# A selective scan's broadcast rows issued ahead of its state sums, the skip term at step 8, and the gate multiply ahead of step 2's multiply

## The reference

```
dt = softplus(einsum('blr,dr->bld', dt, W_dt) + b_dt)
dA = exp(dt[..., None] * A)                        # b, s, 256, 16
dBu = dt[..., None] * Bm[:, :, None, :] * u[..., None]
h_t = dA_t * h_{t-1} + dBu_t                       # a scan over s
y_t = einsum('bdn,bn->bd', h_t, C_t)               # sum over the 16 states
y = (y + u * Dvec) * silu(z)                       # skip term, gate
out = einsum('bld,od->blo', y, W_out)
```

## Time and profile before

| | |
|---|---|
| three runs | 1035.14, 1037.38, 1037.41 us, median 1037.38 |
| profiled execution | 1034.91 us |
| its span | 1032.6 us |
| mean granted clock of TensorE, share of 2.4 GHz | 0.848 |
| the scans of the two layers | first scan starts at 254.7 and 547.3 us, last one ends at 484.8 and 780.1 us |
| VectorE busy in the span | 687.2 us (67%) |
| largest entry of the chain that ended last | TensorE `ps` line 883, 6%; VectorE `hs_all` line 1306, 6% |

### The profile page before, as it was taken

The page is one execution under the profiler, slowest core; times in us unless marked ns, Lnnn a source line. Parts: engine busy times, 40 slices in busy tenths (PEclk is TensorE's granted clock), DMA queues, the critical chain, the costliest instruction groups (busy, mean ns, idle before and its releaser), DMA issues.

```text
span 1032.6 us, 9533 instructions
## 1 busy us (share of the span) xinstructions
PE 739.0 (72%) x2718; PEld 408.9 (40%) x2718; DVE 687.2 (67%) x823; ACT 489.7 (47%) x890; POOL 490.2 (47%) x242
## 2 busy tenths in 40 slices
PE   3773756683876777687866677777774419999998
PEld 2342444420322223232212222232331319989887
DVE  5733687474988888977548988979796591133332
ACT  1413232476754646553776645646461202245554
POOL 6102663101998888978007988979783000000000
PEclk8755786786889999999966989999999556799999
DMA  3000000000000000000000000000004000000000
GB/s 143 1 0 3 1 1 1 0 0 1 0 0 1 0 0 0 0 0 0 1 1 0 1 0 1 0 0 0 0 1 162 0 1 1 1 11 2 10 10 10
DMA packets 2688, 9.37 MB, mean 9 GB/s; under 512 B 697, under 2 KB 826, under 8 KB 2018
## 3 DMA queue, kind: packets, MB, share of 16 engines
q1 hardware_dynamic: 2658, 9.00, 2.3%
HBM read 7.95 MB, written 1.05 MB: 9 GB/s over the span
## 4 chain that ended last, share of the span: by engine, by line
PE 41%; DVE 27%; issue 12%; ACT 10%; POOL 9%; DMA 0%; DVEq 0%; ACTq 0%; POOLq 0%; SPq 0%
PE ps L883 6%; DVE hs_all L1306 6%; DVE ps L1291 5%; POOL hc_all L442 4%; PE ps L975 3%; PE ps L1009 3%; PE ps L999 3%; PE ps L991 3%; ACT ps L633 2%; PE ps L877 2%; PE ps L889 2%; ACT da L633 2%; POOL dbu L429 2%; PE ps L845 1%; DVE big L1108 1%
## 5 line engine op out<-in xcount | busy, mean ns | idle before, releaser
L883 PE MATMUL ps<-hc_all,ident 128*128 128x512 f32 x512 | 257.8, 628 | 34.7 <-POOL hc_all L442 34.2
L442 POOL TENSOR_TENSOR hc_all<-hs_all,c_row 128x1024 f32<-128x1024 f32 x88 | 210.5, 2392 | 37.8 <-DVE hs_all L1306 16.1
L883 PEld LDWEIGHTS ps<-hc_all,ident 128*128 128x128 f32 x512 | 99.9, 200 | 140.9 <-issue 84.5
L630 ACT COPY c_row<-ps 128x512 f32<-128x512 f32 x128 | 74.9, 585 | 141.2 <-PE ps L910 123.6
L1306 DVE TENSOR_TENSOR_SCAN hs_all<-da,ps 128x1024 f32<-128x1024 f32 x48 | 109.7, 2286 | 15.2 <-ACT da L633 10.7
L1291 DVE TENSOR_TENSOR ps<-big,ps 128x1024 f32<-128x1024 f32 x88 | 107.4, 1221 | 16.8 <-PE ps L904 7.3
L633 ACT ACTIVATE da<-big,a_neg 128x511 f32 (+1 forms) x176 | 117.2, 716 | 0.0
L1306 DVE TENSOR_TENSOR_SCAN hs_all<-ps,dbu 128x1024 f32<-128x1024 f32 x40 | 91.0, 2275 | 22.2 <-POOL hc_all L442 15.7
L442 POOL TENSOR_TENSOR hc_all<-w_ffn,c_row 128x1024 f32<-128x1024 f32 x40 | 94.1, 2352 | 22.7 <-DVE w_ffn L1306 21.6
L1381 DVE SCALAR_TENSOR_TENSOR big<-ps,slot_of,big 128x512 f32<-128x512 f32 x32 | 24.0, 750 | 110.2 <-ACT big L698 107.8
L429 POOL TENSOR_TENSOR dbu<-big,w_mod 128x1024 f32<-128x1024 f32 x40 | 96.2, 2404 | 0.0
(11 more groups left out here) (250 smaller groups left out, 1241.6 us busy)
## 6 DMA issues: line engine op xcount, KB each, us to landing
tmpA<-w_in SPq DMA_DIRECT2D x2, 1024.0 KB, 7.0
tmpB<-w_in SPq DMA_DIRECT2D x2, 1024.0 KB, 9.0
x_tok<-x_in SPq DMA_DIRECT2D x1, 1024.0 KB, 7.0
out<-x_tok SPq DMA_DIRECT2D x4, 256.0 KB, 2.1
w_mod<-w_mod_in SPq DMA_DIRECT2D x1, 768.0 KB, 4.9
w_ffn<-w_ffn_in SPq DMA_DIRECT2D x1, 560.0 KB, 7.7
w_in<-w_in_in SPq DMA_DIRECT2D x1, 512.0 KB
w_attn<-w_attn_in SPq DMA_DIRECT2D x1, 320.0 KB, 7.3
```

What stands on the lines that cost most here:

```text
L442: nc.gpsimd.tensor_tensor(hc[:, n % 4, :, :], hs3[HS_BUF[n]].rearrange("p (i s) -> p i s", i=IC), c_row[:, n % 4, :].unsqueeze(1).to_broad ...
L630: nc.scalar.copy(c_row[:, n % 4, :], ps[:, CB, :]).then_inc(c_cs, 1)
L883: mm = nc.tensor.matmul(ps[:, YS + i, :], ident[:], hc[:, n % 4, i, :], start=False, stop=(n == NS - 1))
```

## The change

Four things are edited. `LAG` goes from 3 to 2, so a state sum stands one step earlier. In a step that has a share row, this row (now line 914) is made ahead of the step's state sum and no longer behind it. The skip term goes from step 3, ahead of the sum of state 0, to step 8, behind the sum of state 6, and the sum of state 0 now starts the banks (`start=(n == 0)`). On VectorE the gate multiply goes from behind the multiply of step 2 to ahead of it. The work is the same in kind and number.

```diff
--- before.py
+++ after.py
@@ -187,10 +187,10 @@
         y_sb = sb("y_sb", [P, IC, S])
         h1T = xn[:].rearrange("p t d -> p (t d)")
         DT_AT = [4, 8, 12]
-        LAG = 3
+        LAG = 2
         SHARE = [3, 6, 9, 12, 15]
         NORMAL = [n for n in range(NS) if n not in SHARE]
-        ROWS_AHEAD, INC_AHEAD, OUT_AT, Y_AT = 3, 3, 5, 2
+        ROWS_AHEAD, INC_AHEAD, OUT_AT, Y_AT, SKIP_AT = 3, 3, 5, 2, 8
         DA_BUF = {n: i % 2 for i, n in enumerate(NORMAL)}
         HS_BUF = [n % 3 for n in range(NS - 1)] + [1]
         b_row = w_mod[:, :, 0:S]
@@ -874,13 +874,13 @@
                 def add_skip(b):
 
                     for i in range(IC):
-                        nc.tensor.matmul(ps[:, YS + i, :], diag_d[:, l * IC + i, :], uT[:, b, i, :], start=True, stop=False)
+                        nc.tensor.matmul(ps[:, YS + i, :], diag_d[:, l * IC + i, :], uT[:, b, i, :], start=False, stop=False)
 
                 def add_state(at, n):
 
                     pe.wait_ge(c_hc, at + 1)
                     for i in range(IC):
-                        mm = nc.tensor.matmul(ps[:, YS + i, :], ident[:], hc[:, n % 4, i, :], start=False,
+                        mm = nc.tensor.matmul(ps[:, YS + i, :], ident[:], hc[:, n % 4, i, :], start=(n == 0),
                                               stop=(n == NS - 1))
                     mm.then_inc(c_sum, 1)
 
@@ -909,18 +909,19 @@
                             after(pe, c_cs, at)
                         nc.tensor.matmul(ps[:, CB, :], row_sel[:, NS + n, :], bc_parts[:, b, :], start=True,
                                          stop=True).then_inc(c_cb, 1)
+                        if n + ROWS_AHEAD in SHARE:
+                            pe.wait_ge(c_cs, at + 1)
+                            nc.tensor.matmul(ps[:, CB, :], row_sel[:, n + ROWS_AHEAD, :], bc_parts[:, b, :], start=True,
+                                             stop=True).then_inc(c_cb, 1)
                         if n == LAG:
 
                             after(pe, c_y, l * B + b)
-                            add_skip(b)
                         if n >= LAG:
                             add_state(at - LAG, n - LAG)
                         elif not isinstance(b, int):
                             add_state(at - LAG, NS + n - LAG)
-                        if n + ROWS_AHEAD in SHARE:
-                            pe.wait_ge(c_cs, at + 1)
-                            nc.tensor.matmul(ps[:, CB, :], row_sel[:, n + ROWS_AHEAD, :], bc_parts[:, b, :], start=True,
-                                             stop=True).then_inc(c_cb, 1)
+                        if n == SKIP_AT:
+                            add_skip(b)
                         if n == OUT_AT and not isinstance(b, int):
 
                             pe.wait_ge(c_y, l * B + b)
@@ -1283,6 +1284,8 @@
                 for b in turns(dve, B):
                     for n in range(NS):
                         at = NS * (l * B + b) + n
+                        if n == Y_AT and not isinstance(b, int):
+                            gate_y(b)
                         if n in NORMAL:
                             if n == 0:
                                 dve.wait_ge(q["m_dtu"], b + 1)
@@ -1291,8 +1294,6 @@
                             v.tensor_tensor(ps[:, DBU:DBU + IC, :], dtuT[:, b, :, :],
                                             ps[:, BB, :].unsqueeze(1).to_broadcast([P, IC, S]),
                                             ALU.mult).then_inc(c_bm, 1)
-                        if n == Y_AT and not isinstance(b, int):
-                            gate_y(b)
                         dve.wait_ge(c_da, at + 1)
                         after(dve, c_hc, at - HS_SINCE[n] + 1)
                         if n in NORMAL:
```

## The result

The changed kernel is slower: a median of 1069.53 us (four runs, 1065.9 to 1070.42) against 1036.26 us before (four runs, 1034.98 to 1037.41), a ratio of 1.0315 with a 95% interval of 1.0286 to 1.0344. The direction was forecast, the size was not: +33 us where +13 stood, outside the range. Its profiled execution took 1069.85 us, with a span of 1067.6 us, 35.0 more than before.

The account below looks back on a forecast made before the run. Waits between engines bound the kernel, VectorE setting the turn. Three turns of +2.48 (+7.4), falls gone -3.4, turn 0 into 1 +2.4: +6.5 a layer, +12.9 in all, forecast 1049 us, range 1036 to 1058.

Parts of the forecast that it names:

- the term of `LAG` 2: Scan 13 in each loop turn: rows now behind a sum awaiting GpSimd, worked out as 0.85 us late, taken as 0.75.
- I charge neither: Steps 10 and 0: same `LAG` 2 pattern, taken as hidden in the waits of scans 9 and 13; unhidden about 0.5 each.
- the fall behind the gate multiply: TensorE idles about 3.2 us there, so its clock falls nearly always; 1.2 us charged in all three loop turns.
- The 5.40 us: Scan 3's start after the gate multiply's start, at full clock; VectorE there after 4.67, so a new wait of 0.73 us.
- The skip term at step 8: Skip term behind the sum of state 6 delays row C of step 9: scan 9 waits 0.96 us a turn.
- Scan 4 and multiply 4: Their waits end: 1.36 us back in each of three turns, 1.69 us in the two turns with a clock fall.
- The 0.2 us for the hand-over at scan 2: Scan 2 directly follows its multiply, at 1.34 instead of 1.13 us behind the gate multiply: +0.2 us a turn.
- Turn 0 into turn 1: Rows of the next step 0 stand behind the sum of state 13: scan 0 +2.4 us a layer, +0.7 at full clock.
- the 58.2 that 55.72 + 2.48 would give: A loop turn: the profiled 55.72 us from gate multiply to gate multiply, plus the predicted +2.48 us.
- the waits pile up: Rival: every fall costs 1.9 us and steps 10 and 0 pay too; +10 us, about 1059 us, chance 0.15.

Follow-up runs that it names:

- e5: The kernel before with only the share row moved ahead of the step's state sum: 1033.96 us in ten runs, 0.9968.
- e6: The kernel before with only the skip term moved to step 8 and the sum of state 0 starting the banks, `LAG` 3: 1022.11 us, 0.9872.
- e7: The kernel before with only the gate multiply moved ahead of multiply 2: 1023.45 us, 0.9876.
- e1: The changed kernel with `LAG` back at 3, the other three edits kept: 1024.56 us, 0.9885 of the kernel before.
- e9: e4 with row C of step 2 also repeated eight more times, so TensorE is busy ahead of the gate multiply: 1049.02 us, 1.0141.
- e4: The changed kernel with the share row of step 12 made seven times and row C of step 15 nine times, same values: 1060.18 us, 1.0237.
- e3: The changed kernel with the skip term at step 10 in place of 8: 1070.6 us, 1.0340 of the kernel before.
- e2: The kernel before with `LAG` set to 2 and nothing else changed: 1101.0 us, 1.0637.
- e8: The changed kernel with `LAG` back at 3 and the output projection moved from the end of step 5 to that of step 6: 1025.11 us, 0.9895.
- e10: The changed kernel with `LAG` back at 3 and row C of step 6 made at the end of step 5, ahead of the output projection: 1017.62 us, 0.9805.
- e11: The kernel before with the edits of e6 and e7 and e10's early row C; share rows stay behind the sums, `LAG` 3: 1023.28 us, 0.9889.

## Why the prediction was right in direction and wrong in size

All kernels by their turns 1 to 3, in us:

| kernel | layer 0 | layer 1 | median |
|---|---|---|---|
| before | 167.0 | 169.6 | 1036.3 |
| e5 share row alone | 162.3 | 166.5 | 1034.0 |
| e6 skip term alone | 159.6 | 164.9 | 1022.1 |
| e7 gate alone | 160.3 | 162.9 | 1023.5 |
| e1 all but `LAG` | 160.3 | 163.3 | 1024.6 |
| e9 the change, clock kept up throughout | 168.5 | 172.4 | 1049.0 |
| e4 the change, clock kept up at two sums | 175.4 | 177.3 | 1060.2 |
| the change | 181.6 | 179.7 | 1069.5 |
| e3 the change, skip term at step 10 | 178.7 | 181.6 | 1070.6 |
| e2 `LAG` alone | 191.3 | 190.2 | 1101.0 |
| e8 e1, projection at step 6 | 166.7 | 160.5 | 1025.1 |
| e10 e1, early row C of step 6 | 155.9 | 158.6 | 1017.6 |
| e11 e10, share rows behind the sums | 159.6 | 162.4 | 1023.3 |

**The step that failed is the term of `LAG` 2**, with its companion that the clock falls only behind the gate multiply and at the end of turn 0. The prediction read a wait for a late product as a wait alone: "0.85", "I take 0.75", and at steps 10 and 0 "I charge neither". The position was sized well: 0.76 us at scan 13 with the clock kept up (e4, e9), and also in the two turns of the change in which the clock did not fall there (4.28 us behind scan 12). But in these waits TensorE idles, the clock falls in most of them, and the sum that has just been put ahead of the rows takes 1.7 us longer. Scan 13 therefore paid 2.46 where the clock fell (4 turns of 6), and scan 0 1.3 to 2.0 where nothing had been charged. At step 10 to charge nothing was right (3.55 us, 3.52 before). That the place of the rows makes the difference is to be seen in e1, where the clock still falls and no scan is late for it.

**Scan 3 and the fall behind the gate multiply.** The 5.40 us were right (5.41 in e9). That the fall would come nearly always was right (6 of 6). Its price at scan 3 was 1.7 us and not 1.2 in four turns, where it began with the sum; in the other two it was 1.1 and 1.4.

**The skip term at step 8** made scan 9 wait 1.23 us and not 0.96. The sum ahead of it took 1.82 us and not 1.72, and VectorE was there 0.18 sooner, since scan 7 no longer waited. At `LAG` 3 the skip term costs 0.17 us a turn (e1) or nothing (e6), so the term belongs to the pair.

**Scan 4 and multiply 4** came out as said: no waits (3.55 us), -1.36 and -1.69, but for the first turn of layer 0, where a late fall left 5.01 us. The share of each edit was not what I thought: e7 does it alone, and so does e6 where the clock stays up, so in the change they are paid for once. The 0.2 us for the hand-over at scan 2 did not appear (4.67 us from scan 1 to scan 2 before and after): the gate multiply also starts 0.19 us sooner behind a scan than the multiply did before it, which the sum left out. In e1 and e7 these are 4.90 us, with `LAG` 3.

**Turn 0 into turn 1** was +3.1 and +2.5 against +2.4. Inside turn 0 it was +1.1 in place of nothing. e1, with 57.4, puts this down to `LAG` 2, but it isn't shown: turns 0 of 58.9 and 59.2 us come with `LAG` 3 too (e5). What lies ahead of the first scan and between the layers (+2.5) is not the change's: e6 and e7, which are faster, have the same 66.6 us between the layers.

**The account of a turn** of layer 0 (390.03 to 451.47 us, 61.44, against the 58.2 that 55.72 + 2.48 would give): fall at scan 3 +0.51, scan 9 +0.27, scan 13 +1.71, scan 0 +1.32, hand-over -0.19, scan 15 -0.25 and scan 7 -0.18, which makes 3.19 of the 3.24. e9 splits the 37.7 us between e1 and the change in turns 1 to 3 in two: 20.4 for the falls and 17.2 for the position. With the repeats' own 0.37 us a turn, 2.2 in all, moved from the one to the other, these are about 22.6 and 15, an estimate. The rival "the waits pile up" was right that more steps pay, but bounded the price at 1.0 us more a turn by leaving the clock out of it.

What stays open: why the stretch at 1.2 GHz comes at the sum of state 10 in only four of six turns, with like waits ahead of it (0.68 and 1.34 us in a turn without it).

## What to carry to other kernels

In an engine's list, a wait for a slow producer should stand behind whatever a faster engine needs next; a sum that nobody awaits can be late for free, and the two numbers to compare are its earliest start and that of the row behind it. When an instruction is moved into a wait, price the instruction at TensorE's lower clock too, in every wait and not only in the one behind which it was seen to fall. Edits that end the same wait don't add up: try each alone before adding up their gains.

## What the hardware showed

**The clock falls after short idles.** Before the sum of state 10 TensorE idled for 0.68 and 1.35 us with a row between, and then ran the sum at 0.51 of the full clock, four turns in six; 14 short matmuls a turn put ahead of two of these waits bought 9.4 us of 1069.5. The Trainium skill (TensorE: Matmul & The Clock Gate, "A second HAM failure mode: psum-queue depth-cycling") tells of a kernel in which small idles between groups of matmuls make the clock swing between the two levels. The trace agrees: in turn 2 of layer 0 there are three falls, behind idles of 2.93, 1.35 and 2.65 us. The last idle alone doesn't decide: ahead of the skip term 1.35 us came with a fall in three turns of six (e5) and 1.31 us in none (e7).

**Identical code has two lengths.** Nothing ahead of the loops differs between these kernels, yet the first scan starts at 254.5 to 255.7 us in eight profiles and at 259.8 to 260.7 in five. The window of 200 to 250 us of the kernel before:

```profile
200.00:250.00 50.00, 36.25 (x66) 10.98 (x66) 27.68 (x42) 36.44 (x54) 0.00 (x0) 0.84 0.00 0
```

The mean clock is 0.84 there, and 0.77 in the same window of e1, which is one of the five. It is 0.77 in all five and 0.83 or 0.84 in all eight; why is open. Behind the last scan the same code takes 249.8 to 255.0 us. Such steps of 5 us are the size of the two groups of e5 and of the spread of e10, so a gain below 0.5% in a kernel like this is better read from the loops' own rows.
